# Layer 0 of a two-layer attention block: projection with two image buffers, V stored straight to its column strips

## The chip, the cores and the metric

The kernel runs on one core of a Trainium2 chip: TensorE (matmuls, clock 1.2 or 2.4 GHz as granted), VectorE, ScalarE, GpSimd, and SyncE (SP), which issues most DMAs. The metric is the time of one execution on the device in microseconds, the median of several. The profile shows one execution.

## What is computed

x is [4, 56, 56, 256]: four images of 3136 tokens with 256 channels. Layer 0 is a neighbourhood attention with 8 heads, queries and keys of rank 4, values of 32 channels per head and windows of 7 by 7; layer 1 is a full attention and a mixture of 8 experts.

```python
x = x + _L0_conv_ref(_gn(x), ...)        # group norm over 32 groups of 8 channels
...
q = (x @ Wq + bq).reshape(B, nh, H, W, lr) * scale
k = (x @ Wk + bk).reshape(B, nh, H, W, lr)
v = (x @ Wv + bv).reshape(B, nh, H, W, hd)
```

The reshape takes the 3136 x 32 numbers of an image as [8, 56, 56, 4] without moving them, so a head's grid is cut from 392 consecutive tokens: a token's channels are eight neighbouring columns (SUB = 8 times 4 for Q and K, 8 times 32 for V). Then softmax over the 49 neighbours with a relative bias, the mix with V, and a projection.

## The kernel before

Seven stages follow one another, each a block of its own, with a barrier between them. The change is in the first two.

`layer0_project` loops over four images with hardware loops (`Fori`). For each image SP loads x into one buffer `xs` (L170). TensorE turns it in 14 units of four transposes (L199), ScalarE copies each unit from PSUM into `xT` (L231), VectorE takes statistics of each (L247). Two tiny matmuls with the group matrix (L205) average over groups, VectorE and ScalarE make the inverse root (L62, L70, L64), and VectorE normalises `xT` in place in two instructions (L261). Then TensorE makes Q and K in 7 groups of 448 tokens (L211), which VectorE scales and splits into a high and a low part (L267, L270, L271; the high part is fp32r, and the later products use both), and V in 32 pieces of 98 tokens (L220), to which VectorE adds the bias (L275) into `vs`. SP stores Q/K as two arrays of 64 rows (L173, L174), V into `scratch_v` (L178), waits for all of it, and raises `image_done`, for which TensorE, ScalarE and VectorE wait at the end of the loop's body. Then it issues 14 copies inside HBM (L184) from `scratch_v` to `scratch_vw`: for each half of the heads and each of 7 overlapping strips of 14 columns, the strip's 56 rows of 7168 bytes. The load of the next image's x stands behind them in the same queue.

Beside this GpSimd writes the bias tables with DMAs of its own: fills of 9 MB with a huge number (L130), 24 small ones (L141), and 126 copies of window pieces (L153). Only attention reads these.

`layer0_attend` makes 8 iterations (two halves of the heads, four images) of 28 blocks. An iteration's Q and K are loaded by 32 DMAs (L350, L352) of 4 partitions x 8 pieces of 1568 bytes; GpSimd casts them into `qp` and `kp` (L414, L417). In the head of the stage GpSimd clears `qn` and `kn` (L420, L421), SP loads Q and K, the first biases (L364), the first values (L359) and then the identity `idn` (L402), for which TensorE waits before its first matmul (L440).

Of the kernel before, what the change touches and what calls it, by code (L numbers as in the profile page):

```python
# [6 lines left out]
F32 = mybir.dt.float32  # L7
# [3 lines left out]
ALU = mybir.AluOpType  # L11
# [5 lines left out]
N = H * W  # L17
# [55 lines left out]
def layer0_project(nc, A, S):  # L73
# [4 lines left out]

    with ExitStack() as ctx:
# [3 lines left out]
        def sem(name):  # L83
            return ctx.enter_context(nc.semaphore("p0_" + name))

        idn = sb("idn", [TT, TT])
        blk = sb("blk", [128, 128])
        wqk = sb("wqk", [128, CC, 64])
# [4 lines left out]
        xs = sb("xs", [TT, NT, C])  # L93
        xT = sb("xT", [128, CC, N])
# [6 lines left out]
        tmp = sb("tmp", [64, 2, GW])  # L101
# [9 lines left out]
        consts, loaded, turned, copied = sem("consts"), sem("loaded"), sem("turned"), sem("copied")  # L111
        stat, grouped, normed, chain = sem("stat"), sem("grouped"), sem("normed"), sem("chain")
        qk_made, qk_read, qk_split = sem("qk_made"), sem("qk_read"), sem("qk_split")
        v_made, v_read, stored, image_done = sem("v_made"), sem("v_read"), sem("stored"), sem("image_done")
        spread, rooted = sem("spread"), sem("rooted")
        rpb_loaded, filled = sem("rpb_loaded"), sem("tables_ready")
        tables_written, relaid, steps = sem("tables_written"), sem("relaid"), sem("steps")
        CHAIN = 5 + NG
        VT = 32
# [4 lines left out]
        def _(pool):  # L124
            pool.wait_ge(filled, 1)
# [7 lines left out]
            pool.wait_ge(filled, 2)  # L133
# [23 lines left out]
        @block.sync  # L157
        def _(sp):
            sp.dma_start(rp[:, :], A["rpb"].rearrange("h a b -> (h a) b")).then_inc(rpb_loaded, 16)
            for dst, src in ((idn[:, :], A["eye"][0:TT, 0:TT]), (blk[:, :], A["group_mean"]),  # L160
                             (wqk[:, :, 0:32], A["Wq0"].rearrange("(c p) n -> p c n", p=128)),
                             (wqk[:, :, 32:64], A["Wk0"].rearrange("(c p) n -> p c n", p=128)),
                             (wv[:, :, :], A["Wv0"].rearrange("(c p) n -> p c n", p=128)),
                             (bqk[0:32, :], A["bq0"].rearrange("(p a) -> p a", a=1)),
                             (bqk[32:64, :], A["bk0"].rearrange("(p a) -> p a", a=1)),
                             (sqk[:, :], A["qk_scale"]),
                             (bvb[:, :], A["bv0"].rearrange("(a n) -> a n", a=1).to_broadcast([TT, C]))):
                sp.dma_start(dst, src).then_inc(consts, 16)
            with sp.Fori(0, B) as b:
                sp.dma_start(xs[:, :, :], A["x"][b].rearrange("(j p) c -> p j c", p=TT)).then_inc(loaded, 16)  # L170

                sp.wait_ge(qk_split, (b + 1) * NG)
                sp.dma_start(S["qk0"][b, 0], qkh[:, :].bitcast(F32)).then_inc(stored, 16)  # L173
                sp.dma_start(S["qk0"][b, 1], qkl[:, :].bitcast(F32)).then_inc(stored, 16)  # L174
                for g in range(2):
                    sp.wait_ge(v_read, b * VT + 16 * (g + 1))
                    sp.sem_inc(steps, 1)
                    sp.dma_start(S["v0"][b, g].rearrange("(m t s) d -> t m (s d)", m=4, s=SUB), vs[:, 4 * g:4 * g + 4, :])\  # L178
                      .then_inc(stored, 16)
                sp.wait_ge(stored, (b + 1) * 64)  # L180
                sp.sem_inc(image_done, 1)
                for g in range(2):
# [4 lines left out]
            sp.wait_ge(relaid, B * 2 * COL_BLOCKS * 16)  # L187

        @block.tensor
        def _(pe):  # L190
            pe.wait_ge(consts, 144)
            with pe.Fori(0, B) as b:
                pe.wait_ge(loaded, (b + 1) * 16)
                for k in range(CC * NG):
                    g, c = divmod(k, CC)
                    if k >= 4:
                        pe.wait_ge(copied, b * (CC * NG) + k - 3)
                    for u in range(4):
                        last = pe.transpose(PS[:, k % 4, TT * u:TT * u + TT], xs[:, 4 * g + u, 128 * c:128 * c + 128],  # L199
                                            idn[:, :])  # L200
                    last.then_inc(turned, 1)

                for w, what in enumerate((mv[:, :, 0], vv[:, :])):
                    pe.wait_ge(stat, b * 2 + w + 1)
                    pe.matmul(PS[:, 4 + w, 0:CC], blk[:, :], what, start=True, stop=True).then_inc(grouped, 1)  # L205
                pe.wait_ge(normed, (b + 1) * CC)
                for g in range(NG):
                    if g >= 4:
                        pe.wait_ge(qk_read, b * NG + g - 3)
                    for c in range(CC):  # L210
                        last = pe.matmul(PS[0:64, g % 4, 0:GW], wqk[:, c, :], xT[:, c, GW * g:GW * g + GW],  # L211
                                         start=(c == 0), stop=(c == CC - 1))
                    last.then_inc(qk_made, 1)
                for j in range(VT):
                    if j >= 4:
                        pe.wait_ge(v_read, b * VT + j - 3)
                    g, m, hh = j // 16, j // 4 % 4, j % 4
                    tok = HT * (4 * g + hh) + 98 * m
                    for c in range(CC):
                        last = pe.matmul(PS[0:98, 4 + j % 4, 0:C], xT[:, c, tok:tok + 98], wv[:, c, :],  # L220
                                         start=(c == 0), stop=(c == CC - 1))
                    last.then_inc(v_made, 1)
                pe.wait_ge(image_done, b + 1)

        @block.scalar
        def _(act):
            with act.Fori(0, B) as b:
                for k in range(CC * NG):
                    g, c = divmod(k, CC)
                    act.wait_ge(turned, b * (CC * NG) + k + 1)  # L230
                    act.activation(xT[:, c, GW * g:GW * g + GW], PS[:, k % 4, 0:GW], ACT.Copy).then_inc(copied, 1)  # L231
                root(act, rstd[:, :], spread, rooted, b + 1)
                act.wait_ge(image_done, b + 1)

        @block.vector
        def _(dve):
            dve.memset(idle[:, :], 0.0)
# [3 lines left out]
            dve.wait_ge(consts, 144)  # L241
            with dve.Fori(0, B) as b:
                ch = Count(dve, chain, b * CHAIN)
                for k in range(CC * NG):
                    g, c = divmod(k, CC)
                    dve.wait_ge(copied, b * (CC * NG) + k + 1)
                    last = dve.bn_stats(stats[:, c, g, :], xT[:, c, GW * g:GW * g + GW])  # L247
                ch.after(last)
                dve.tensor_copy(idle[:, 1:2], idle[:, 0:1])
                for c in range(CC):  # L250
                    last = dve.bn_aggr(mv[:, c, :], stats[:, c, :, :].rearrange("p g s -> p (g s)"))
                last.then_inc(stat, 1)
                dve.wait_ge(grouped, b * 2 + 1)
                ch.after(dve.tensor_copy(gm[:, :], PS[:, 4, 0:CC]))
                ch.after(dve.tensor_tensor(dd[:, :], mv[:, :, 0], gm[:, :], ALU.subtract))
                ch.after(dve.tensor_tensor(dd[:, :], dd[:, :], dd[:, :], ALU.mult))
                dve.tensor_tensor(vv[:, :], dd[:, :], mv[:, :, 1], ALU.add).then_inc(stat, 1)
                dve.wait_ge(grouped, b * 2 + 2)
                inverse_root(dve, ch, rstd[:, :], PS[:, 5, 0:CC], 1e-5, spread, rooted, b + 1)
                for c in range(CC):  # L260
                    dve.tensor_scalar(xT[:, c, :], xT[:, c, :], gm[:, c:c + 1], rstd[:, c:c + 1],  # L261
                                      ALU.subtract, ALU.mult).then_inc(normed, 1)
                for g in range(NG):
                    dve.wait_ge(qk_made, b * NG + g + 1)
                    t = tmp[:, g % 2, :]

                    dve.tensor_scalar(t, PS[0:64, g % 4, 0:GW], bqk[:, 0:1], sqk[:, 0:1], ALU.add, ALU.mult)\  # L267
# [1889 lines left out]
```

## Time and profile before

| | us |
|---|---|
| median of 3 runs | 7947.33 (7942.66 to 7951.0) |
| profiled execution, its own time | 7931.02 |
| its span in the trace | 7929.2 |
| projection of layer 0 (0 to 443.9) | 443.9 |
| head of attention, to its first matmul (443.9 to 490.2) | 46.3 |
| rest of attention (490.2 to 1324.0) | 833.8 |

A stretch of the trace is read like this: busy time of each engine, the share of full speed at which TensorE's clock was granted, the mean busy share of the 16 DMA engines, and what they moved. An "x" after an instruction is a count; records of one run of instructions are merged in the timeline, so a duration there is that of the run.

### The profile page before, as it was taken

The numbers are of one execution on the slowest core, as the hardware profiler recorded it, in microseconds if no ns is written. First come the engines' busy times: TensorE is split into PE (matmuls) and PEld (weight loads), VectorE is DVE, ScalarE is ACT, GpSimd is POOL, SyncE is SP. The second block draws the span as 40 slices with busy tenths as digits, with TensorE's granted clock in tenths as the row PEclk, the third lists the DMA queues.
The fourth block names the chain that finished last, engine by engine and source line by source line (L and its number), as shares of the span: only waits on it lengthen the run. The fifth ranks groups of instructions, "written<-read, shape, count | busy, mean of one in ns | idle before, by whom it ended". The sixth has DMA issues, their size and how long they took to land. (4 is left out here: it accounts for less than half of the span.)

```text
span 7929.2 us, 152182 instructions
## 1 busy us (share of the span) xinstructions
PE 7120.8 (90%) x47408; PEld 4323.5 (55%) x47408; DVE 5376.1 (68%) x12877; ACT 4022.7 (51%) x9367; POOL 3714.0 (47%) x2395
## 2 busy tenths in 40 slices
PE   4459998989999999999999999999999888709999
PEld 2347776655455455455455455455455334608888
DVE  3359997659977677677677677677677102618888
ACT  0049997220055655565565555555565664104444
POOL 4011111110066666666666666666666665365554
PEclk8779999995599999999999999999999999859999
DMA  5442323871001201211211211211211102611221
GB/s 158 137 118 68 98 70 93 253 234 44 13 23 30 64 24 38 58 26 36 57 34 28 60 36 26 57 35 33 59 30 37 28 3 67 205 33 56 62 57 31
DMA packets 403136, 519.85 MB, mean 66 GB/s; under 512 B 64096, under 2 KB 355474, under 8 KB 399063
## 3 DMA queue, kind: packets, MB, share of 16 engines
q1 hardware_dynamic: 379687, 469.02, 21.9%
q0 software_dynamic: 22640, 40.75, 1.9%
q8 instruction: 421, 6.90, 0.4%
q14 instruction: 388, 3.18, 0.1%
HBM read 339.07 MB, written 200.10 MB: 68 GB/s over the span
## 5 line engine op out<-in xcount | busy, mean ns | idle before, releaser
L1248 DVE TENSOR_REDUCE a_tops<-a_ps 128x1 f32<-128x448 f32 (+1 forms) x5600 | 3071.8, 612 | 1092.9 <-PE a_ps L1150 1075.2
L1371 POOL TENSOR_TENSOR a_added<-a_P 128x896 f32<-128x896 f32 x1344 | 2799.3, 2102 | 2095.8 <-ACT a_P L1348 2095.8
L1348 ACT ACTIVATE a_P<-a_ps 128x448 f32<-128x448 f32 (+1 forms) x5600 | 2656.6, 547 | 2123.5 <-PE a_ps L1219 2081.9
L1219 PE MATMUL a_ps<-a_qp,a_kp 98*128 98x448 f32 (+1 forms) x5600 | 2154.1, 400 | 104.2 <-ACT a_P L1348 77.2
L1150 PE MATMUL a_ps<-a_hk,a_hq 96*128 96x448 f32 (+1 forms) x4900 | 1818.4, 381 | 2.0 <-DMA a_hq<-scratch_q 1.9
L1219 PEld LDWEIGHTS a_ps<-a_qp,a_kp 98*128 98x128 f32 (+1 forms) x5600 | 1028.9, 187 | 1296.0 <-ACT a_P L1348 741.0
L1170 PE MATMUL a_ps<-a_P,a_vt 128*32 128x448 f32 (+1 forms) x11200 | 1335.1, 549 | 0.0
L1150 PEld LDWEIGHTS a_ps<-a_hk,a_hq 96*128 96x128 f32 (+1 forms) x4900 | 916.4, 187 | 263.6 <-DVE a_tops L1248 170.3
L1186 PE MATMUL a_ps<-a_added,a_ones 128*32 128x448 f32 x5376 | 649.0, 555 | 0.0
L1170 PEld LDWEIGHTS a_ps<-a_P,a_vt 128*32 128x32 f32 (+1 forms) x11200 | 290.1, 109 | 513.9 <-issue 386.4
L550 ACT ACTIVATE n_P<-n_sm,n_mx 112x280 f32<-112x280 f32 x896 | 467.9, 522 | 108.4 <-DVE n_mx L498 108.3
L1271 DVE RECIPROCAL a_sums<-a_sums 128x112 f32<-128x112 f32 x224 | 185.0, 835 | 488.8 <-ACT a_sums L1323 488.8
L451 PE MATMUL n_ps<-n_idn,n_P 112*98 112x112 f32 x2688 | 421.2, 267 | 10.2 <-DVE n_P L508 10.2
L448 PE MATMUL n_ps<-n_idn 112*112 112x112 f32 x1792 | 373.1, 291 | 30.7 <-ACT n_PTs L557 29.8
L498 DVE CUSTOM_DVE_ANT_0 n_sm<-n_ps,n_bias 112x280 f32<-112x280 f32 x896 | 349.2, 445 | 72.3 <-PE n_ps L440 48.7
L557 ACT ACTIVATE n_PTs<-n_ps 98x336 f32<-98x336 f32 x896 | 391.1, 437 | 2.6 <-PE n_ps L451 2.0
L1138 PE MATMUL a_ps<-a_kp,a_qp 96*128 96x448 f32 (+1 forms) x700 | 370.2, 726 | 22.4 <-DMA a_kp<-scratch_k 22.4
L414 POOL CAST n_qp<-n_qn 128x784 fp32r<-128x784 f32 x32 | 52.5, 1639 | 673.7 <-DMA n_kn<-scratch_qk 338.2
L508 DVE TENSOR_SCALAR n_P<-n_P,n_rc 112x280 f32<-112x280 f32 x896 | 334.2, 415 | 16.0
L1951 ACT ACTIVATE e_h<-e_ps,e_b 128x512 f32<-128x512 f32 (+1 forms) x256 | 172.0, 672 | 336.2 <-PE e_ps L1911 311.8
L1924 PE MATMUL e_ps<-e_w2h,e_hTh 128*128 128x256 f32 (+1 forms) x1024 | 295.4, 289 | 37.0 <-DVE e_widest L2033 37.0
L448 PEld LDWEIGHTS n_ps<-n_idn 112*112 112x112 f32 x1792 | 255.4, 183 | 112.5 <-ACT n_PTs L557 98.9
(195 smaller groups left out, 7787.2 us busy)
## 6 DMA issues: line engine op xcount, KB each, us to landing
a_qp<-scratch_q SPq DMA_DIRECT2D x168, 224.0 KB, 3.9
a_kp<-scratch_k SPq DMA_DIRECT2D x96, 320.0 KB, 5.5
a_hk<-scratch_k SPq DMA_DIRECT2D x84, 336.0 KB, 5.0
scratch_t<-o_ts SPq DMA_DIRECT2D x56, 448.0 KB, 5.5
scratch_vw<-scratch_v SPq DMA_DIRECT2D x56, 392.0 KB
n_vt<-scratch_vw SPq DMA_DIRECT2D x64, 343.0 KB
a_hq<-scratch_q SPq DMA_DIRECT2D x84, 200.0 KB, 3.2
e_w<-in_w SPq DMA_DIRECT2D x16, 1024.0 KB, 7.1
```

The lines of the kernel that those rows point to most:

```text
L448: pe.matmul(PS[0:TT, turn_bank(m), 384:384 + TT], idn[:, :], idn[:, :], start=True, stop=True)
L451: last = pe.transpose(PS[0:CHUNK, turn_bank(m), TT * c:TT * c + TT], P[:, m % RP, k0:k0 + CHUNK], idn[:, :])
L550: act.activation(P[:, m % RP, :], sm[:, m % 4, :], ACT.Exp, bias=mx[:, m % 8:m % 8 + 1], scale=-1.0, accum_out=rs[:, m % 8:m % 8 + 1]).the ...
L557: act.activation(PTs[:, m % 8, :], PS[0:CHUNK, turn_bank(m), 0:3 * TT], ACT.Copy).then_inc(copied, 1)
L1138: pe.matmul(PS[0:rows_of(t), i % FIRST_BANKS, 0:GW], qp[0:96, hh, 128 * t:128 * t + rows_of(t)], kp[0:96, hh, GW * k:GW * k + GW], start=T ...
L1150: pe.matmul(PS[0:rows_of(t), MAX + i % MAXES, 0:GW], hq[:, 128 * t:128 * t + rows_of(t)], hk[:, GW * k:GW * k + GW], start=True, stop=True ...
L1170: last = pe.matmul(PS[HD * hh:HD * hh + HD, MIX, 0:GW], vt[0:rows, t, HD * hh:HD * hh + HD], P[0:rows, (2 * n + hh // 2) % (2 * RING), hh ...
L1186: last = pe.matmul(PS[HD * hh:HD * hh + HD, SUM, 0:GW], ones[:, :], added2[:, (2 * (PAIRS * j + u) + hh // 2) % 6, hh % 2, :], start=(u == ...
L1219: pe.matmul(PS[0:rows_of(t), i_s % 3, 0:GW], kp[0:98, hh, 128 * t:128 * t + rows_of(t)], qp[0:98, hh, GW * j:GW * j + GW], start=True, sto ...
L1248: dve.tensor_reduce(tops[0:rows_of(t), KT * hh + t, k:k + 1], PS[0:rows_of(t), bank, 0:GW], AX_X, ALU.max).then_inc(topped, 1)
L1348: act.activation(P[0:rows_of(t), (2 * n + pair) % (2 * RING), hh % 2, :], PS[0:rows_of(t), (4 * n + hh) % 3, 0:GW], ACT.Exp).then_inc(expe ...
L1371: pool.tensor_tensor(added2[:, a % 6, :, :], P[:, (2 * n + pair) % (2 * RING), :, :], P[:, (2 * n + 2 + pair) % (2 * RING), :, :], ALU.add ...
```

## The change

In `layer0_project` the loops over images are written out, and the images overlap. `xs` and `xT` have two buffers each. TensorE, ScalarE and VectorE go through 39 items per image (7 groups of Q/K, 32 pieces of V), and between an image's items stand the transposing units of the next (at odd items), its statistics (items 28 to 34) and its normalising (items 35 and 36). The transposes have two PSUM banks, Q/K two, V three. ScalarE makes the high part of Q/K (Identity with bias), VectorE the low part in one instruction. The scale goes into the weights once, and the weights' columns are put in another order, so that Q/K rows come out by rank component first. Q/K are stored by five DMAs of 32 rows (Q: high, low; K: high, low, high), V by 19 DMAs for each half of the heads, from `vs` straight into the strips; `scratch_v` is not used here any more. Each load of x is two DMAs. GpSimd begins its tables when image 0 is there. At the end the semaphores are cleared and a barrier is added. No engine waits for a whole image to be stored: ScalarE and VectorE wait for the stores of the buffer that they write next.

In `layer0_attend` Q and K come by 16 DMAs of 8 rows, the identity is loaded first, `qn` is cleared by VectorE while GpSimd clears `kn`, and the first loads of Q/K and biases don't wait for the clearing of `vt`.

```diff
@@ layer0_project
-        xs = sb("xs", [TT, NT, C])
-        xT = sb("xT", [128, CC, N])
+        xs = sb("xs", [TT, 2, NT, C])
+        xT = sb("xT", [128, 2, CC, N])
...
         def _(pool):
-            pool.wait_ge(filled, 1)
+            pool.wait_ge(filled, 2)
+            for h in range(2):
+                pool.wait_ge(loaded[0][h], 16)
...
+            def load(b):
+                if b >= 2:
+                    sp.wait_ge(turned, UNITS * (b - 1))
+                for h, (j0, j1) in enumerate(HALVES):
+                    sp.dma_start(xs[:, b % 2, j0:j1, :], A["x"][b, TT * j0:TT * j1, :].rearrange("(j p) c -> p j c", p=TT))\
+                      .then_inc(loaded[b % 2][h], 16)
+            def store_qk(b):
+                sp.wait_ge(qk_split, NG * (b + 1))
+                for qk in range(2):
+                    rows = slice(32 * qk, 32 * qk + 32)
+                    for term in range(2 + qk):
+                        src = (qkh, qkl)[term % 2]
+                        sp.dma_start(S["qk0"][b, qk, :, term].rearrange("h c s t -> (c s) h t"),
+                                     src[rows, :].rearrange("p (h t) -> p h t", h=NH).bitcast(F32)).then_inc(qk_stored, 16)
+            def store_values(b, g):
+                sp.wait_ge(v_read, b * VT + 16 * (g + 1))
+                for tc, xb, s0, s1, at in STRIP_PARTS:
+                    sp.dma_start(S["vw"][b, g, tc].rearrange("(m r c) d -> r m (c d)", m=4, c=14)
+                                 [:, :, 128 * at:128 * (at + s1 - s0)],
+                                 vs[xb:98:COL_BLOCKS, 4 * g:4 * g + 4, 128 * s0:128 * s1]).then_inc(v_stored[g], 16)
...
+            load(1)
+            for b in range(B):
+                if b + 2 < B:
+                    load(b + 2)
+                store_qk(b)
                 for g in range(2):
-                sp.wait_ge(stored, (b + 1) * 64)
-                sp.sem_inc(image_done, 1)
-                    for tc in range(COL_BLOCKS):
-                        sp.dma_start(S["vw"][b, g, tc].rearrange("(r c) d -> r c d", c=14),
-                                     S["v0"][b, g].rearrange("(r c) d -> r c d", c=W)[:, KEY_COL[tc]:KEY_COL[tc] + 14, :])\
-                          .then_inc(relaid, 16)
+                    store_values(b, g)
...
+            for b in range(B):
+                pe.wait_ge(normed, CC * (b + 1))
+                for n in range(ITEMS):
+                    if n < NG:
+                        queries_and_keys(b, n)
+                    else:
+                        value(b, n - NG)
+                    if b + 1 < B:
+                        if n % 2 == 1 and n < 2 * UNITS:
+                            turn(b + 1, n // 2)
+                        if n == 30:
+                            group(b + 1, 0)
+                        if n == 32:
+                            group(b + 1, 1)
...
+            def high_of(b, g):
+                n = NG * b + g
+                if g == 0 and b > 0:
+                    act.wait_ge(qk_stored, 16 * 5 * b)
...
+            def value(b, j):
+                n = VT * b + j
+                if j % 16 == 0 and b > 0:
+                    dve.wait_ge(v_stored[j // 16], V_STORES * b)
...
+    nc.clear_and_free_semaphores(sems)
+    nc.all_engine_barrier()
@@ layer0_attend
-                    for term in range(4):
-                        rows = slice(32 * hh + 4 * term, 32 * hh + 4 * term + 4)
-                        sp.dma_start(qn[rows, :, :], S["qk0"][b, term // 2, 0:32, tok:tok + HT]
-                                     .rearrange("(s c) t -> c s t", c=LR)).then_inc(loaded, 16)
...
+                    for half in range(2):
+                        rows = slice(32 * hh + 8 * half, 32 * hh + 8 * half + 8)
+                        sp.dma_start(qn[rows, :, :], S["qk0"][b, 0, 4 * g + hh, 0:2].rearrange("e c s t -> (e c) s t"))\
+                          .then_inc(loaded, 16)
...
-            sp.wait_ge(zeroed, 3)
+            sp.dma_start(idn[:, :], A["eye"][0:TT, 0:TT]).then_inc(consts, 16)
+            sp.wait_ge(zeroed, 2)
             load_qk(0, 0)
             load_bias(0, 0)
+            sp.wait_ge(padded, 1)
             load_values(0, 0, 0)
-            sp.dma_start(idn[:, :], A["eye"][0:TT, 0:TT]).then_inc(consts, 16)
```

## Rows read from the trace of the kernel before

**Rows 1.** Stretches: start:end, length, busy time, clock, DMA share, GB/s.
```profile
core 0: us, PE busy (x) PEld busy (x) DVE busy (x) ACT busy (x) POOL busy (x), PEclk, DMA share, GB/s
0.00:50.80 50.80, 0.00 (x0) 0.00 (x0) 2.25 (x3) 1.28 (x1) 9.54 (x16) 1.00 0.83 255
...
256.80:322.40 65.60, 49.46 (x216) 33.63 (x216) 38.25 (x78) 8.24 (x16) 0.00 (x0) 0.86 0.25 73
322.40:357.00 34.60, 0.04 (x1) 0.04 (x1) 0.00 (x0) 1.28 (x1) 0.00 (x0) 0.50 0.85 255
...
443.90:490.20 46.30, 0.02 (x4) 0.02 (x4) 1.55 (x1) 1.28 (x1) 14.39 (x9) 0.50 0.47 110
490.20:1324.00 833.80, 789.37 (x10644) 629.43 (x10645) 765.02 (x3352) 768.89 (x2678) 93.73 (x58) 0.96 0.29 76
```
**Rows 2.** Waits, 0 to 480 us: in total, times, longest.
```profile
PE p_ps L199 <- DMA p_xs<-in_x: 182.7, 4, 50.8
```
**Rows 3.** Groups of instructions by line and shape, 0 to 900 us.
```profile
L153 POOL DMA_DIRECT2D scratch_bias<-scratch_toeplitz x126 | 72.7, 586 | 10.8 <-issue 9.4 <-DMA scratch_toeplitz<-p_rn 1.4
L275 DVE TENSOR_TENSOR p_vs<-p_ps,p_bvb 98x256 f32<-98x256 f32 x128 | 53.1, 422 | 48.3 <-PE p_ps L220 48.3
...
L247 DVE BATCH_NORM_STATS2 p_stats<-p_xT 128x6 f32<-128x448 f32 x56 | 31.8, 617 | 186.5 <-ACT p_xT L231 184.2
...
L261 DVE TENSOR_SCALAR p_xT<-p_xT,p_gm,p_rstd 128x3136 f32<-128x3136 f32 x8 | 14.9, 1909 | 0.1
```
**Rows 4.** Timeline of the projection: start, duration, engine, line, count.
```profile
4.55 7.38 POOL L130 DMA_DIRECT2D scratch_bias<-p_far  x8
...
50.82 8.34 PE L199 MATMUL p_ps<-p_idn,p_xs 112*128 112x112 f32 x56 [50.82 <-DMA p_xs<-in_x]
...
68.09 13.45 PE L211 MATMUL p_ps<-p_xT,p_wqk 128*64 128x448 f32 x28 [4.46 <-DVE p_xT L261]
...
81.47 27.87 PE L220 MATMUL p_ps<-p_wv,p_xT 128*98 128x256 f32 x128
...
360.25 4.96 ACT L231 ACTIVATE p_xT<-p_ps 128x448 f32<-128x448 f32 x11 [0.20 <-PE p_ps L199]
...
373.89 12.45 PE L211 MATMUL p_ps<-p_xT,p_wqk 128*64 128x448 f32 x28 [4.46 <-DVE p_xT L261]
```
**Rows 5.** Short stretches: Q/K store, V store, x load, first Q/K load.
```profile
85.50:92.00 6.50, 6.50 (x32) 4.98 (x31) 3.29 (x8) 0.00 (x0) 0.68 (x2) 1.00 1.06 222
97.00:102.50 5.50, 5.50 (x28) 4.18 (x27) 2.58 (x7) 0.00 (x0) 5.50 (x11) 1.00 0.90 294
...
345.00:356.00 11.00, 0.00 (x0) 0.00 (x0) 0.00 (x0) 0.00 (x0) 0.00 (x0) 0.50 0.99 239
...
449.00:468.00 19.00, 0.00 (x0) 0.00 (x0) 0.00 (x0) 0.00 (x0) 0.35 (x1) 0.50 0.25 62
```
**Rows 6.** SP's issues by line: min/median/max of one in ns.
```profile
L178 SPq DMA_DIRECT2D scratch_v<-p_vs x8: 327/348/388, 96.2 to 414.9; - x8
...
L184 SPq DMA_DIRECT2D scratch_vw<-scratch_v x56: 798/802/982, 118.5 to 436.1; - x56
...
L350 SPq DMA_DIRECT2D n_qn<-scratch_qk x128: 249/404/1709, 449.4 to 1153.0; - x128
```
**Rows 7.** The next stage's high and low parts: min/median/max in ns.
```profile
L766 ACT ACTIVATE o_high<-o_ps,o_bqk x112: 633/633/636, 1370.7 to 1763.1; 128x448 fp32r<-128x448 f32 x112
L823 DVE SCALAR_TENSOR_TENSOR o_low<-o_ps,o_bqk,o_high x112: 670/682/685, 1371.4 to 1763.8; 128x448 fp32r<-128x448 f32 x112
```
**Rows 8.** Timeline of attention's head.
```profile
444.00 2.71 POOL L420 MEMSET n_qn<- 128x3136 f32 x1 [298.01 <-POOLq L79]
...
449.38 0.28 SPq L350 DMA_DIRECT2D n_qn<-scratch_qk  x1
...
481.17 1.57 POOL L414 CAST n_qp<-n_qn 128x784 fp32r<-128x784 f32 x1 [31.81 <-DMA n_kn<-scratch_qk]
...
483.35 1.83 SPq L402 DMA_DIRECT2D n_idn<-in_eye  x1
...
490.18 0.58 PE L440 MATMUL n_ps<-n_kp,n_qp 16*112 16x280 f32 x4 [76.03 <-DMA n_idn<-in_eye]
```

More of the change, by code:

```diff
@@ L73, in layer0_project @@
 def layer0_project(nc, A, S):
+    sems = []
     with ExitStack() as ctx:
@@ L83, in sem @@
         def sem(name):
-            return ctx.enter_context(nc.semaphore("p0_" + name))
+            sems.append(nc.alloc_semaphore("p0_" + name))
+            return sems[-1]
+        UNITS = CC * NG
+        VT = 32
+        ITEMS = NG + VT
+        TURN, MEAN, QK, VAL = 0, 2, 3, 5
         idn = sb("idn", [TT, TT])
         blk = sb("blk", [128, 128])
+        raw = sb("raw", [128, CC, 64])
         wqk = sb("wqk", [128, CC, 64])
@@ L189, in _ @@
+            for g in range(2):
+                sp.wait_ge(v_stored[g], V_STORES * B)
+            sp.wait_ge(qk_stored, 16 * (B * 5))
         @block.tensor
         def _(pe):
[L191 to L223, printed above, removed]
@@ new lines, in turn @@
+            def turn(b, k):
+                g, c = divmod(k, CC)
+                if k == 0:
+                    pe.wait_ge(loaded[b % 2][0], 16 * (b // 2 + 1))
+                if k == CC * 4:
+                    pe.wait_ge(loaded[b % 2][1], 16 * (b // 2 + 1))
+                if b * UNITS + k >= 2:
+                    pe.wait_ge(copied, b * UNITS + k - 1)
+                for u in range(4):
+                    last = pe.transpose(PS[:, TURN + k % 2, TT * u:TT * u + TT], xs[:, b % 2, 4 * g + u, 128 * c:128 * c + 128],
+                                        idn[:, :])
+                last.then_inc(turned, 1)
@@ new lines, in group, with queries_and_keys @@
+            def group(b, w):
+                pe.wait_ge(stat, b * 2 + w + 1)
+                pe.matmul(PS[:, MEAN, CC * w:CC * w + CC], blk[:, :], (mv[:, :, 0], vv[:, :])[w], start=True, stop=True)\
+                    .then_inc(grouped, 1)
+            def queries_and_keys(b, g):
+                n = NG * b + g
+                if n >= 2:
+                    pe.wait_ge(qk_split, n - 1)
+                for c in range(CC):
+                    last = pe.matmul(PS[0:64, QK + n % 2, 0:GW], wqk[:, c, :], xT[:, b % 2, c, GW * g:GW * g + GW],
+                                     start=(c == 0), stop=(c == CC - 1))
+                last.then_inc(qk_made, 1)
@@ new lines, in value @@
+            def value(b, j):
+                n = VT * b + j
+                if n >= 3:
+                    pe.wait_ge(v_read, n - 2)
+                g, m, hh = j // 16, j // 4 % 4, j % 4
+                tok = HT * (4 * g + hh) + 98 * m
+                for c in range(CC):
+                    last = pe.matmul(PS[0:98, VAL + n % 3, 0:C], xT[:, b % 2, c, tok:tok + 98], wv[:, c, :],
+                                     start=(c == 0), stop=(c == CC - 1))
+                last.then_inc(v_made, 1)
@@ new lines, in _ @@
+            pe.wait_ge(consts, CONSTS)
+            for k in range(UNITS):
+                turn(0, k)
+            group(0, 0)
+            group(0, 1)
+            pe.wait_ge(prepared, PREPARED)
+            for b in range(B):
[12 more added lines that the diff above has]
+                            group(b + 1, 1)
@@ L225, in _, with take_turned @@
         @block.scalar
         def _(act):
[L227 to L233, printed above, removed]
+            def take_turned(b, k):
+                g, c = divmod(k, CC)
+                act.wait_ge(turned, b * UNITS + k + 1)
+                act.activation(xT[:, b % 2, c, GW * g:GW * g + GW], PS[:, TURN + k % 2, 0:GW], ACT.Copy).then_inc(copied, 1)
@@ L235, in _, with collect @@
+            for b in range(B):
+                for n in range(ITEMS):
+                    if n < NG:
+                        high_of(b, n)
+                    if b + 1 < B:
+                        if n % 2 == 1 and n < 2 * UNITS:
+                            take_turned(b + 1, n // 2)
+                        if n == 33:
+                            root(act, rstd[:, :], spread, rooted, b + 2)
         @block.vector
         def _(dve):
+            ch = Count(dve, chain, 0)
+            def collect(b, k):
+                g, c = divmod(k, CC)
+                dve.wait_ge(copied, b * UNITS + k + 1)
+                last = dve.bn_stats(stats[:, c, g, :], xT[:, b % 2, c, GW * g:GW * g + GW])
+                if k == UNITS - 1:
+                    ch.after(last)
@@ new lines, in means, with spreads @@
+            def means(b):
+                dve.tensor_copy(idle[:, 1:2], idle[:, 0:1])
+                for c in range(CC):
+                    last = dve.bn_aggr(mv[:, c, :], stats[:, c, :, :].rearrange("p g s -> p (g s)"))
+                last.then_inc(stat, 1)
+            def spreads(b):
+                dve.wait_ge(grouped, b * 2 + 1)
+                ch.after(dve.tensor_copy(gm[:, :], PS[:, MEAN, 0:CC]))
+                ch.after(dve.tensor_tensor(dd[:, :], mv[:, :, 0], gm[:, :], ALU.subtract))
+                ch.after(dve.tensor_tensor(dd[:, :], dd[:, :], dd[:, :], ALU.mult))
+                dve.tensor_tensor(vv[:, :], dd[:, :], mv[:, :, 1], ALU.add).then_inc(stat, 1)
@@ new lines, in variances, with invert, normalise @@
+            def variances(b):
+                dve.wait_ge(grouped, b * 2 + 2)
+                dve.tensor_scalar(rstd[:, :], PS[:, MEAN, CC:2 * CC], 1e-5, None, ALU.add).then_inc(spread, 1)
+            def invert(b):
+                dve.wait_ge(rooted, b + 1)
+                ch.after(dve.reciprocal(rstd[:, :], rstd[:, :]))
+            def normalise(b, c):
+                dve.tensor_scalar(xT[:, b % 2, c, :], xT[:, b % 2, c, :], gm[:, c:c + 1], rstd[:, c:c + 1],
+                                  ALU.subtract, ALU.mult).then_inc(normed, 1)
@@ new lines, in _ @@
+            dve.tensor_tensor(bqk[:, :], bqk[:, :], sqk[:, :], ALU.mult).then_inc(prepared, 1)
+            dve.wait_ge(prepared, PREPARED)
+            invert(0)
+            for c in range(CC):
+                normalise(0, c)
+            for b in range(B):
+                for n in range(ITEMS):
+                    if n < NG:
+                        low_of(b, n)
+                    else:
+                        value(b, n - NG)
+                    if b + 1 < B:
+                        if n % 2 == 1 and n < 2 * UNITS:
+                            collect(b + 1, n // 2)
+                        if n == 28:
+                            means(b + 1)
+                        if n == 30:
+                            spreads(b + 1)
+                        if n == 32:
+                            variances(b + 1)
+                        if n == 34:
+                            invert(b + 1)
+                        if n in (35, 36):
+                            normalise(b + 1, n - 35)
```

140 lines of the change are left out of this document (68 added, 72 removed).

## Prediction

> **What bounds the kernel now.** I read the stretches of the span first [rows 1]. The change touches the first 490 us only: projection from 0 to 443.9, and the head of attention, until TensorE's first matmul at 490.2. The rest of attention (833.8 us, TensorE busy 789, ScalarE 769, VectorE 765) and all after it keep their code. The projection alternates: a stretch with no DMA to speak of (256.8 to 322.4, 65.6 us, DMA share 0.25) and one in which every engine stands still and only DMAs run (322.4 to 357.0, 34.6 us, 0.04 us of matmuls, DMA share 0.85). Nothing overlaps, because `image_done` holds TensorE, ScalarE and VectorE until V is stored, and the next image is loaded behind the 14 copies of V into strips. The waits say the same: TensorE waited 182.7 us for `p_xs` over four images [rows 2], and 76.0 us before the first matmul of attention [rows 8]. So the stage is bound by a chain of latencies, and what decides is which engine or queue is the longest when an image's work overlaps the next one's.
>
> **The time before the first projection.** Before, the 8 fills of the bias tables (9.0 MB) go out at 4.55 us, x (3.2 MB) behind them, and TensorE starts at 50.8 [rows 1, 4]. Now GpSimd waits for image 0. 3.21 MB of x at the 239 GB/s that a load alone got [rows 5] are 13.4 us; from an issue at 1.7, with 2 us of latency, 17 us; the constants are queued behind it (0.5 MB, 2 us): TensorE starts at 19 (17 to 23). From there to the first Q/K matmul it was 68.09 - 50.82 = 17.3 us [rows 4]. Two PSUM banks for the transposes instead of four let TensorE run only one unit ahead of ScalarE's copy, and scaling the weights adds five tiny instructions: I add 1.5 us (0.5 to 3). First Q/K matmul at 37.8.
>
> **One image in the steady state, engine by engine.** TensorE: 28 Q/K records; at the full clock one takes its place every 0.373 us (image 3 did 28 in 12.45 us with a part at the low clock; image 0 13.45) [rows 4], so 10.4 us. V: 128 records in 27.87 us, 0.218 apart [rows 4]. The 14 transposing units: 11 copies of them ran in 4.96 us once the clock was up, 0.45 each [rows 4], so 6.3. Statistics matmuls 0.9. 28 changes between the kinds of work, at 0.05 us as an estimate, 1.4 (0 to 3). VectorE: 14 x 0.617 statistics, 2 x 1.909 normalising, 7 x 0.68 for the low parts (the nearest row is the same operation in the next stage), 32 x 0.422 V, 2 us of small ones: 32.7 us [rows 3, 7]. Three of its instructions a Q/K group become one, and ScalarE takes the high part at 0.63 [rows 7]. ScalarE: 14 x 0.45 + 7 x 0.63 = 10.7 us and two table loads. So TensorE is the longest, with one stall that I can place: the two normalising instructions of the next image stand at items 35 and 36 of VectorE's order. From TensorE's end of item 35, VectorE needs 0.2 + 2 x (0.42 + 1.91) = 4.9 us before `normed` is full; TensorE has three more values of 0.87 us, so it stands for 2.3 us. Sum: 10.4 + 27.9 + 6.3 + 0.9 + 1.4 + 2.3 = 49.2 us. In the Q/K phase two banks return in 0.63 + 0.68 + some 0.4 of semaphores = 1.7 us, within the 1.9 us of a matmul group and a transposing unit; no stall.
>
> **Is the queue longer?** An image is x 3.21 MB at 239 GB/s = 13.4 us; Q and K, now five stores of 0.40 MB, 2.0 MB at the 222 GB/s that the 64-row stores got = 9.0; V written straight, 7 strips x 56 rows x 7168 bytes x 2 = 5.62 MB, at the 294 GB/s of the V store [rows 5] 19.1 us. Together 41.5 us, against 49.2 of TensorE: hidden, with 8 us to spare. The rows know no store that reads only 14 partitions. From below it is the 294; from above the pace of the slowest load here: the first Q/K load of attention, 1.6 MB over a quarter of the DMA engines (share 0.25), took 449.4 to 481.2 [rows 5, 8], 12.6 GB/s per engine; at that, 14 engines give 177 GB/s, 31.8 us, and the queue comes to 54.2. I take 294, since the V store is nearest (SBUF to HBM, rows of 4 KB against now 1.5 to 4 KB). Issuing: 38 strip stores an image; the V store took 0.35 us to issue, a strip copy 0.80 [rows 6]. At 0.5 this is 19 us of SP, at 0.8 it is 30: below 49 either way.
> A rule speaks against the narrow stores. The Trainium skill, "SBUF — State Buffer", section on Door 1, says that a DMA's rate goes by how many of 16 ports its partitions reach, and that rows 0 to 63 reach no more than 0 to 31. The trace agrees with the half rate for 64 rows (222 GB/s at full DMA share), and by the rule 32 rows cost no more: the 9.0 us stand.
>
> **Order of waits.** SP now queues per image: load(b+2), five Q/K stores, 19 strip stores, 19 more. load(b+2) waits for the transposes of image b, done before image b's items begin, so nothing is held up behind it. ScalarE's `high_of(b+1, 0)` waits for Q/K stores issued some 36 us earlier; VectorE's value(b+1, 0) for strips issued some 27 us earlier that need 10. Image 1 is the tight one: x(1) shares the DMA with the 9 MB of fills. In that company 3.2 MB of x were there only at 50.8 before, some 44 us for them [rows 1, 4]; now x(1) runs from about 17, so its first half is there at some 40, when the first transposing unit wants it (37.8 + 3), and the second at 61, when unit 8 does. GpSimd's 126 small copies (72.7 us of its time before, [rows 3]) follow the fills and 24 smaller ones and end near 155, hidden by the stage. No stall taken; 0 to 8 us as bounds.
>
> **The stage.** 37.8; image 0 49.2 + 3.0 for the low clock of its first matmuls [rows 4] = 90.0; two more 49.2 = 188.4; the last has no next image, 10.4 + 27.9 + 0.5 = 38.8: 227.2. Then 19 strip stores (2.8 MB, 9.6 us of data, 9.5 of issue) and landing, 14 us together (9 to 20, at 0.35 to 0.8 a store, plus what queues before them): 241.2. Clearing semaphores and one more barrier: 1.5 (0 to 3): 242.7. Before 443.9: a gain of 201.2.
>
> **Head of attention.** Before, 46.3 us: two memsets of GpSimd (5.4), 32 loads, casts from 481.2, and only then the identity, issued at 483.4 behind biases and values, which TensorE waited for [rows 8]. After: one memset per engine (2.7 plus 0.3), 16 loads of 8 rows. 4-row loads kept a quarter of the DMA engines busy; 8-row loads should use half, so 1.6 MB take between 9.5 (21 GB/s per engine, as in the V store) and 31.8 us (no gain); I take 13, as rows of 12.5 KB replace pieces of 1568 bytes. Four casts of at most 1.57 are 5.8 us. TensorE is ready at 3.2 + 13 + 5.8 = 22; the biases, whose four loads are next in the queue, at about 23. Gain 23.3 (5 to 28).
> The Trainium skill, "DMA: Bandwidth & Descriptors", section on why a DMA increments its semaphore by 16, says that the engine count divides the slowest dimension, 4 then and 8 now; the share of 0.25 agrees. The rule on ports, taken by itself, would give 8 rows two ports of 27 GB/s, 30 us, and with it the second rival's time; 4 rows would then have had one, and 62 GB/s was measured [rows 5].
>
> **Sum.** 201.2 + 23.3 = 224.5 us. The profiled execution took 7931.0 (7929.2 in the span) and would take 7706.5; the timed runs had a median of 7947.3, 16 above, so 7723.
>
> **Rivals.** (1) The strip stores run slower than the V store, the queue becomes the bound: 54.2 instead of 49.2 for three images, in the tail 6 us more, and bubbles between waits and issue, 5 us an image: 15 + 6 + 15 = 36 more, 7759. For it: source rows on only 14 partitions. Against: 14 DMA engines already carried the V store. (2) The head's load is no faster: 18 us more, 7742. For it: it was slower in the head than its engines' share explains. (3) Slower than before: an overlapped stage waits for its strips at every image. The whole gain of 224 us over four images is 56 each, so an image must take 105 us, and a strip store (105 - 13.4 - 9.0)/38 = 2.2 us instead of 0.5; it decides from there. Only the worst issue of a 49 KB load comes near, 1.71 us, and its median is 0.40 [rows 6]. At 2.5 us each: 38 x 0.3 x 4 = 46 more than before, 7993. (4) The overlap doesn't come about, TensorE waiting each image for VectorE's normalising and the transposes: 65 us an image, 3 x 16 = 48 more, 7771; nothing in the order asks for it.
>
> **Chances.** Forecast 0.57, (1) 0.20, (2) 0.14, (4) 0.06, (3) 0.03. A change within 0.2% (16 us), about what this kernel's timing can't tell from none, has no case of its own: 0.01. Faster 0.96, slower 0.03. Range: down to 7697 (head 5, tail 5, changes of work and start 8, runs 8); up to 7780, which takes in (1) with (2) in part, and (4). The forecast's own: 7700 to 7745.
>
> **What would show it.** First transposes at 19 us; images 49 us apart at the Q/K matmuls; TensorE's only regular wait 2.3 us on VectorE's normalising; DMA share near 0.85; attention's first matmul 22 to 24 us after its memset; attention from there still 834 us. Wrong would be: TensorE, ScalarE or VectorE waiting for `qk_stored` or `v_stored`, transposes waiting for x, or a longer attention body.

## The result

The changed kernel took 7744.6 us in the median (7731.4 to 7755.7, four runs) beside 7945.0 before: a ratio of 0.9746 (95% interval 0.9729 to 0.9764), 200 us less. In a second comparison it took 7729.2 (five runs) beside 7935.1: 0.9739 (0.9726 to 0.9753), 206 us less. The forecast of 7723, 224 less, had the direction and lies 22 us under the first median and 6 under the second; both medians lie inside the stated range. The profiled execution took 7755.7 us, span 7753.8, the longest of its four.

The stretches of the changed kernel's profile show where the time came from (columns as in [rows 1]): two images, the last image, the wait for its stores, and the head of attention.

```profile
87.70:134.90 47.20, 45.22 (x216) 30.08 (x216) 30.13 (x65) 11.94 (x22) 43.73 (x74) 1.00 0.87 237
134.90:182.10 47.20, 45.22 (x216) 30.07 (x216) 30.13 (x65) 11.93 (x22) 22.88 (x42) 1.00 0.72 205
182.10:221.90 39.80, 39.03 (x156) 24.45 (x156) 18.88 (x41) 4.40 (x7) 0.00 (x0) 1.00 0.62 182
221.90:247.90 26.00, 0.00 (x0) 0.00 (x0) 0.00 (x0) 0.00 (x0) 0.00 (x0) 0.58 0.47 167
...
247.90:287.50 39.60, 0.00 (x0) 0.02 (x1) 4.22 (x2) 1.28 (x1) 8.68 (x6) 0.50 0.76 100
```

Where a compute stretch of 65.6 us alternated with a DMA stretch of 34.6 [rows 1], an image now takes 47.2 us, TensorE works in 45.2 of them, its clock stays at full speed, and the DMAs run beside it. In the timeline the same kernel's steps show at their edges:

```profile
20.67 4.71 PE L236 MATMUL p_ps<-p_idn,p_xs 112*128 112x112 f32 x24 [20.67 <-DMA p_bqk<-in_bk]
...
39.22 4.55 PE L250 MATMUL p_ps<-p_xT,p_wqk 128*64 128x448 f32 x8 [4.76 <-DVE p_xT L348]
...
87.74 3.22 PE L250 MATMUL p_ps<-p_xT,p_wqk 128*64 128x448 f32 x8 [1.97 <-DVE p_xT L348]
...
182.12 8.14 PE L250 MATMUL p_ps<-p_xT,p_wqk 128*64 128x448 f32 x20 [1.97 <-DVE p_xT L348]
```

The Q/K matmuls of an image begin 48.5, 47.2 and 47.2 us apart. In front of the first image's TensorE waits 4.76 us for VectorE's normalising, in front of each of the other three 1.97 us, and after the first image the projection has no longer wait of TensorE. Then the head of attention, which answers to [rows 8]:

```profile
247.93 2.71 POOL L552 MEMSET n_kn<- 128x3136 f32 x1 [90.15 <-POOLq L410]
...
251.35 0.27 SPq L481 DMA_DIRECT2D n_qn<-scratch_qk  x1
...
281.54 1.57 POOL L546 CAST n_qp<-n_qn 128x784 fp32r<-128x784 f32 x1 [30.89 <-DMA n_kn<-scratch_qk]
...
287.51 0.58 PE L571 MATMUL n_ps<-n_kp,n_qp 16*112 16x280 f32 x4 [66.30 <-POOL n_kp L549]
```

TensorE now waits for the casts (66.3 us, with the tail of the projection in it), not for the identity. But the load still takes 251.4 to 281.5, 30.2 us, where the old one took 31.8. And the strip stores show in SP's issues (min/median/max of one in ns) with a median of 782 ns:

```profile
L195 SPq DMA_DIRECT2D scratch_vw<-p_vs x152: 781/782/2967, 71.1 to 243.9; - x152
```

In time order, SP's issues from image 1's strip stores on look like this:

```profile
121.04 39.56 SPq L195 DMA_DIRECT2D scratch_vw<-p_vs  x38
160.64 0.53 SPq L189 DMA_DIRECT2D scratch_qk<-p_qkh  x1
...
167.86 34.74 SPq L195 DMA_DIRECT2D scratch_vw<-p_vs  x38
...
209.84 34.84 SPq L195 DMA_DIRECT2D scratch_vw<-p_vs  x38
```

SP issues without a gap from 71.1 to 244.7 us. The x load (image 1 only), the five Q/K stores and the 38 strip stores take it 55.7 us for image 1 and 42.0 each for images 2 and 3, against TensorE's 47.2. So SP is behind when an image's values end: image 1's last strip store is issued 26 us after TensorE has gone on to image 2's Q/K, and VectorE's first write into the second half of `vs` (165.7) comes only 5 us after the last store of the old contents was issued (160.6). No engine waits for the stores, but with little to spare.

So two questions stand: why the head kept 16.6 us of what was forecast to go, and why the tail took 26 us instead of 15.5.

### The profile page after: what moved, and what is told of

The parts are those of the page before. It is cut to its first block and busy times, and to the rows that moved or that the text cites. A ratio compares the mean times of both kernels' runs of the same rounds, so it can differ in the third digit from the quotient of the medians.

```text
span 7753.8 us, 151401 instructions
## 1 busy us (share of the span) xinstructions
PE 7122.0 (92%) x47408; PEld 4321.3 (56%) x47408; DVE 5352.3 (69%) x12827; ACT 4036.6 (52%) x9389; POOL 3715.9 (48%) x2394
## 3 DMA queue, kind: packets, MB, share of 16 engines
q1 hardware_dynamic: 380887, 457.79, 22.7%
```

## The experiments

All variants start from the changed kernel. Stage times are of one profile each.

**Q/K rows four partitions apart.**

```diff
-                        rows = slice(32 * hh + 8 * half, 32 * hh + 8 * half + 8)
+                        rows = slice(32 * hh + half, 32 * hh + 32, 4)
...
-                    rows = slice(32 * hh, 32 * hh + 16)
+                    rows = slice(32 * hh, 32 * hh + 32)
```

> The changed kernel, but the 8 rows of a Q/K load of attention go to partitions four apart (32 hh + half + 4 j) instead of 8 neighbours, and the score matmuls contract over 32 rows, of which the other 16 are zero. Same bytes, same 8 rows and 16 DMAs. Theory A (the load is held by how few SBUF ports its neighbouring rows reach): the head load, 30.2 us in the changed kernel (251.4 to 281.5), takes 9 to 14 us, and the time from attention's memset to its first matmul falls from 39.6 to 20 to 25 us. Theory B (8 of 16 DMA engines, or the read from HBM, hold it): it stays within 3 us of 30 and the head at 37 to 41. Attention's body must keep its pace in both.

Measured: 7696.4 us in one run (before, beside it: 7930.2). The timeline of this variant:

```profile
253.89 0.69 SPq L481 DMA_DIRECT2D n_qn<-scratch_qk  x1
...
268.20 1.57 POOL L546 CAST n_qp<-n_qn 128x784 fp32r<-128x784 f32 x1 [15.03 <-DMA n_kn<-scratch_qk]
...
274.18 0.58 PE L571 MATMUL n_ps<-n_kp,n_qp 32*112 32x280 f32 x4 [50.95 <-POOL n_kp L549]
```

The load takes 253.9 to 268.2, 14.3 us, and from the memset at 250.5 to the first matmul 23.7. Bytes, number of DMAs and source are those of the changed kernel; for the load only where the rows lie in SBUF differs. (That the matmuls contract over 32 rows doesn't shorten the head: a run below has that edit alone, with a head of 40.2.) The biases and values are queued behind the Q/K loads, in the changed kernel from 256.8 on, so its 30.2 us are in part spent in their company. These stretches lie before that company, from 2 us after the first issue: neighbouring rows, then rows four apart.

```profile
253.40:256.70 3.30, 0.00 (x0) 0.00 (x0) 0.00 (x0) 0.00 (x0) 0.00 (x0) 0.50 0.49 61
```

```profile
255.90:264.30 8.40, 0.00 (x0) 0.00 (x0) 0.00 (x0) 0.00 (x0) 0.00 (x0) 0.50 0.43 143
```

At nearly the same share of busy DMA engines, about 8 of 16, twice as much moves. Theory A stands as far as it says that the place of the rows decides. The Trainium skill, "SBUF — State Buffer", section on Door 1, has four neighbouring partitions share one port of 27 GB/s; by it 8 neighbours reach two, 1.6 MB in 30 us as an estimate, and rows four apart reach eight. The trace agrees with the direction. That the first comes out at 30.2 us is in part luck: of the changed kernel's load, 251.4 to 256.7 moved 76 GB/s with nothing beside it, more than two ports of 27, and the rest ran beside biases and values. Of the 14.3 us, 10.4 are SP's issues, so this run doesn't show what eight ports would give. The issue itself, 0.30 us for neighbouring rows, costs 0.60 with a step:

```profile
L481 SPq DMA_DIRECT2D n_qn<-scratch_qk x64: 602/603/1532, 253.9 to 919.1; - x64
```

**32 loads of 4 neighbouring rows.** The inner loop runs over four terms again, with rows of 12.5 KB.

```diff
-                    for half in range(2):
-                        rows = slice(32 * hh + 8 * half, 32 * hh + 8 * half + 8)
+                    for term in range(4):
+                        rows = slice(32 * hh + 4 * term, 32 * hh + 4 * term + 4)
```

> The changed kernel, but Q and K of attention come by 32 DMAs of 4 neighbouring rows (12.5 KB each) instead of 16 of 8. Theory A (ports): 4 neighbours reach half of what 8 reach, so the head load takes 55 to 62 us and the head some 65 to 70. Theory B (DMA engines, 4 instead of 8): also about twice, 55 to 60. Theory C (the pieces of 1568 bytes were as fast as rows of 12.5 KB, and the old load's 31.8 us are what any such load takes here): 30 to 34 us. With the first kernel this separates rows in memory from rows in SBUF.

Measured: 7728.1 us in one run. The load took 253.9 to 282.4, 28.5 us, the head 37.9. A stretch with Q/K loads alone, then a line of this kernel's timeline:

```profile
255.90:264.60 8.70, 0.00 (x0) 0.00 (x0) 0.00 (x0) 0.00 (x0) 0.00 (x0) 0.50 0.23 53
```

```profile
282.37 1.57 POOL L544 CAST n_qp<-n_qn 128x784 fp32r<-128x784 f32 x1 [29.20 <-DMA n_kn<-scratch_qk]
```

The DMA share is 0.23, half of the 0.49 with 8 rows, and the rate 53 GB/s against 61. Neither A nor B: half the DMA engines and half the neighbours are nearly as fast as twice of each. C's time is nearest. So the forecast's reading of the share 0.25 (twice the DMA engines, and so well under half the time) is wrong in this place: the load was not bound by them. This run answers another rival of the run above too: its 32 issues also take 10.7 us and put the biases off by as much as the stepped issues do, and the load stays at 28.5 us, so the later biases are not what halved it. That ports are what binds is argued, not shown: why 4 rows, which by the same rule have one port, do as well as 8 stays open. A possible reason is that loads of different groups of four are under way at once; no run parts that.

**The last strips from two queues.** First ScalarE issued 28 of the last image's 38 strip stores and SP 10:

```diff
+            for g in range(2):
+                act.wait_ge(v_read, (B - 1) * VT + 16 * (g + 1))
+                for tc, xb, s0, s1, at in (STRIP_PARTS, STRIP_PARTS[1::2])[g]:
+                    act.dma_start(S["vw"][B - 1, g, tc]...
```

> The changed kernel, but of the last image's 38 strip stores ScalarE's queue issues the 19 of the first half and 9 of the second, SP the other 10. Theory A (the tail, 26.0 us from the last value to attention's memset, is bound by SP's issues at 0.82 us each, 29 of them still to go): it falls to 11 to 14 us, the stage ends near 235. Theory B (bound by the data or by DMA engines): it stays within 3 us of 26.

Measured: 7723.5 us in one run; the last value at 220.3 and attention at 239.0, a tail of 18.7 us instead of 26.0. It fell by less than A had it (11 to 14), but well out of B's 3 us. ScalarE's 28 took 29.2 us, 1.04 each, so ScalarE's queue now set the end, with SP done at 231:

```profile
206.54 29.16 ACTq L319 DMA_DIRECT2D scratch_vw<-p_vs  x28
```

Then both queues took every other strip store, in both halves (`STRIP_PARTS[0::2]` and `[1::2]`):

> The changed kernel with the last image's strip stores taken in turns by SP and ScalarE in both halves, and nothing else. The same edit in the kernel with spread rows had its attention memset at 236.7 us, 15.0 after the last value. Expected here 235 to 238, head 38 to 41, and 10 to 12 us less than the changed kernel's 7729.2: 7717 to 7720. If the body's length hangs on when the last strips land, it shows here as well (body under 832).

Measured: 7716.2 us (7703.7 to 7733.4, four runs), ratio 0.9721 (0.9703 to 0.9740) to the kernel before, which took 7937.1. Attention begins at 236.0, a tail of 13.4 after the last value, at 222.6, and the head takes 39.9. The tail was bound by issues. Beside each other the two queues took 22.7 us for 38 stores, 0.60 a store, where SP alone took 34.8. The body of attention (first to last matmul) took 847.0 us, so earlier strips don't shorten it.

**Images in turn.** The transposes, statistics and normalising of an image stand after the previous one's items on every engine, here on TensorE:

```diff
-                    if b + 1 < B:
-                        if n % 2 == 1 and n < 2 * UNITS:
-                            turn(b + 1, n // 2)
...
+            for b in range(B):
+                for k in range(UNITS):
+                    turn(b, k)
```

> The changed kernel with its two buffers, narrow stores and strips, but an image's transposes, statistics and normalising come after the previous image's items, in turn, not between them. It tells what the interleaving is worth beside no longer waiting for stores and loads. Theory A (most of the gain is the DMA waits that went, 35 us an image): an image takes 38.8 + 17 to 18.5 = 56 to 58 us instead of 47.2, the stage ends 27 to 33 us later, near 277. Theory B (the queue would show as soon as the engines have gaps, or the low clock after the gaps costs more): 62 us an image or more, the stage ends after 295.

Measured: 7749.0 us in one run. Attention begins at 276.4. A stretch of 57 us is about an image (columns as in [rows 1]); TensorE works 48.3 of it at a clock of 0.91, in the two stretches behind it as well, and the Q/K matmuls begin 58 us apart (97.3, 155.2, 213.1).

```profile
58.00:115.00 57.00, 48.29 (x213) 30.78 (x213) 31.18 (x63) 11.47 (x22) 42.94 (x74) 0.91 0.84 223
```

Theory A stands. Of the projection's 196 us (443.9 to 247.9), 167 come without any interleaving: 30 of them from the start, where the first transpose comes at 20.6 instead of 50.8, and some 137 mainly from images that no longer wait for stores and loads (TensorE's waits for x after the first were 182.7 - 50.8 = 131.9 us [rows 2]). The interleaving adds 28.5.

**V through HBM, but overlapped.** Two stores and 14 copies inside HBM instead of 38 strip stores:

```diff
-                for tc, xb, s0, s1, at in STRIP_PARTS:
-                    sp.dma_start(S["vw"][b, g, tc]...
+                sp.dma_start(S["v0"][b, g].rearrange("(m t s) d -> t m (s d)", m=4, s=SUB), vs[:, 4 * g:4 * g + 4, :])
...
+            def relay(b, g):
+                sp.wait_ge(v_stored[g], 16 * (b + 1))
+                for tc in range(COL_BLOCKS): ...
```

> The changed kernel with its overlap, but V goes as before: two stores of an image's V to HBM, and 14 copies inside HBM from there into the strips, which SP issues once the store has landed. Theory A (strips straight from SBUF matter little while TensorE sets the pace): images stay 47 to 49 us apart and only the tail changes. Theory B (the extra 3.2 MB and the copies make the queue the bound: x 13.4, Q/K 9.0, V store 11, copies 21.5, together 55 us): images 55 us apart, ScalarE or VectorE waiting for stores or transposes for x, the stage 15 to 25 us longer than the changed kernel's 247.9. The fewer issues (14 at 0.8 and 2 at 0.35 instead of 38 at 0.8) speak for A, the bytes for B.

Measured: 7737.2 us in one run. Q/K matmuls begin at 38.0, 87.5, 134.7 and 183.6: 49.5, 47.2 and 48.9 us apart, and attention at 249.5. The stretches show the price that does not reach the time, a DMA share of 1.00 and 0.87 in images that have 0.87 and 0.72 with strips:

```profile
90.00:137.00 47.00, 45.03 (x214) 29.87 (x213) 30.11 (x64) 11.31 (x21) 36.58 (x62) 0.98 1.00 284
137.00:185.00 48.00, 46.03 (x218) 30.26 (x217) 30.11 (x64) 11.94 (x22) 24.41 (x44) 0.99 0.87 293
```

Theory A: the stage ends 1.6 us later, inside the scatter of profiles of the same projection code (246.6 to 250.5), so the direct strip stores as such are worth nothing that this run shows. They unload the DMA engines; they don't carry the gain. B's 55 us an image didn't come: its terms had rates of 239 to 294 GB/s [rows 5], and these stretches move 284 to 293.

**Tables first.**

```diff
-            for h in range(2):
-                pool.wait_ge(loaded[0][h], 16)
```

> The changed kernel, but GpSimd starts its table fills at once, not when image 0 is there. Theory A (x shares the DMA engines with 9 MB of fills as in the kernel before): the first transpose starts at 38 to 47 us instead of 20.7, and the stage ends by nearly as much later, 265 to 274. Theory B (x is now issued before the fills and keeps ahead of them): 22 to 28 us, and the stage ends within 6 us of 248.

Measured: 7748.7 us in one run. The first transpose starts at 44.0 instead of 20.7, and attention at 270.1 instead of 247.9: 22.2 us for two lines.

```profile
43.97 9.94 PE L234 MATMUL p_ps<-p_idn,p_xs 112*128 112x112 f32 x56 [43.97 <-DMA p_bqk<-in_bk]
```

What TensorE waited for last is the constants, as in the changed kernel, not x. x is issued at 1.6 us and the fills from 4.6 on; the constants are issued behind x until 37.6, where the changed kernel had issued them by 15.8. Theory A's time came, but how much of it is x and how much the constants this run doesn't part.

**Both remedies together, and the changed kernel again.**

> The changed kernel with the Q/K rows of attention four partitions apart and the last image's strip stores taken in turns by SP and ScalarE, in both halves. From the single runs: head 39.6 to 23.7 us, tail 26.0 to 18.5 with an uneven split (ScalarE 28, SP 10); an even split ends both queues at about 231 and the stage at 234 to 236. Sum 28 to 31 us less than the changed kernel's median 7744.6: 7712 to 7718. If the data and not the issues bound the tail by now (share of the DMA engines 0.8 in it), the stage ends at 238 to 240 and the time is 7720.

Measured: 7683.0 us (7680.6 to 7695.1, five runs), ratio 0.9683 (0.9670 to 0.9696) to the kernel before; beside it on the same chip the changed kernel took 7729.2. That is 46 us less, and 62 less than the 7744.6 from which 28 to 31 were expected.

> The changed kernel again, beside the one above on the same chip. Every theory: median within 10 us of 7744.6, stage end 246 to 250, head 38 to 41 us. The length of attention's body (840.7 in the kernel before, 851.4 in the changed one, 828.9 to 839.1 in four variants that leave it alone or nearly) falls between 828 and 852 if that difference is scatter from run to run, and near 851 if it belongs to the change.

Its stage: attention at 246.6, first matmul at 286.4. With both remedies:

```profile
236.71 0.35 SPq L535 DMA_DIRECT2D n_idn<-in_eye  x1
...
260.10 0.58 PE L577 MATMUL n_ps<-n_kp,n_qp 32*112 32x280 f32 x4 [39.02 <-POOL n_kp L555]
```

From 286.4 to 260.1 are 26 us, a little less than expected. In the body of attention, 828.2 us against 842.4, are 14 more. Of the two profiled executions one is 34 us shorter than the other, so the medians' 46 are not accounted for in full. To part the two edits of the spread rows, the 32-row matmuls were run with the neighbouring loads:

> The changed kernel, Q/K loads of attention to neighbouring rows as it has them, but the score matmuls contract over 32 rows, of which 16 are zero. It parts the two edits of the spread kernel, whose attention body took 828.9 and 828.2 us in two profiles, where eight profiles with neighbouring rows gave 832.3 to 851.4. Theory A (the slow Q/K load of the next iteration sits before the values in the queue and makes TensorE late and its clock fall): body 832 to 851, head 38 to 41. Theory B (32 live rows a matmul keep the clock up, or change the pace): body 826 to 831. Time by A within 10 us of 7729, by B some 12 less.

Measured: 7721.9 us (7717.1 to 7736.9, four runs), ratio 0.9732 (0.9716 to 0.9749); body 838.0, head 40.2. So the rows of the matmul don't bring the short body. In the nine profiles with neighbouring rows in the new layout the body took 832.3 to 851.4, in the two with spread rows 828.9 and 828.2. The timed runs speak for the faster load as well: the kernel with both remedies and the one with the even tail alone differ only by the two edits of the spread rows, and their medians by 33 us (7683.0 and 7716.2, no run of one within the range of the other), of which the head explains 16.5. TensorE's waits in the body of the changed kernel's second profile, then of the kernel with both remedies (in total, times, longest):

```profile
PE n_ps L594 <- issue: 3.9, 1, 3.9
PE n_ps L579 <- issue: 2.1, 1, 2.1
```

```profile
PE n_ps L585 <- ACT n_PTs L695: 31.7, 31, 2.1
```

The first has gaps in which TensorE waited for nothing that the profile shows; the second has none. Eight of the nine profiles with neighbouring rows have two or three such gaps, which begin 12 to 30 us after an iteration's Q/K load began to be issued (in this one loads at 404.2 and 718.3, gaps at 421.0 and 735.9). The granted clock over the body is 0.95 in the two longest (851.4 and 847.0) and 0.97 in the two with spread rows. But the slow load alone doesn't make the gaps: the run with 4 rows, whose load takes 28.5 us, has none, a clock of 0.97 and a body of 832.3, and the kernel before had none and a body of 840.7. What makes them stays open.

## Why the prediction was right, and where its terms were off

- *The start of the first image.* 19 forecast, 20.7 measured; Q/K at 37.8 forecast, 39.2 measured. Right, and that the tables wait for image 0 is worth 22 us.
- *An image.* 49.2 forecast, 47.2 measured; the stall 2.3 forecast, 1.97 measured. The working by engines was right. No row stood behind the 1.4 us for 28 changes between kinds of work, and they cost nothing that I can see. The first image took 48.5 instead of 52.2: its low clock cost little, as it ended during the first Q/K groups. The last value came at 221.9, where the sum had 227.2.
- *The queue is hidden.* Right in the outcome: DMA share 0.87 and 0.72, and no engine waits for `qk_stored` or `v_stored`. Rival (1) didn't come. But the 8 us to spare were worked out from bytes. In issues it counted the strip stores alone, 19 to 30 us an image; with the Q/K stores and x SP needed 42.0 to 55.7. The Q/K stores, which were to be issued some 36 us ahead of ScalarE's next write, were issued 16 ahead (167.9 and 183.9), and the stores of the old contents of `vs` 5 ahead of VectorE's.
- *The tail.* The first of two failed terms: 14 and 1.5 us forecast, 26.0 measured, 10.5 too little. The step was "19 strip stores (2.8 MB, 9.6 us of data, 9.5 of issue)": with 0.5 us a store and nothing queued before them, SP would be done with the first half when the last value came. In its place the trace shows SP with 28 of 38 stores to go. They took 23.0 us, 0.82 each, about the upper bound of 0.80 that the prediction had. That price alone would leave some 21 of them: the values of the first half were ready at 207.9 us, but SP still issued image 3's Q/K stores until 209.8 (five in 7.2 us, which the sum had at nothing), and its first ten strip stores then took 11.8 us. From the last issue to attention's memset are 3.2 us, landing, clearing and barriers together; no run parts the 1.5 us forecast for the last two. The even split over two queues gave 12.6 us of the tail back.
- *The head.* The second failed term: 23.3 forecast, 6.7 gained (46.3 to 39.6), 16.6 too little. The failed step is "8-row loads should use half, so 1.6 MB take between 9.5 ... and 31.8 us (no gain); I take 13". It read the share of busy DMA engines as the limit. The engines did double (share 0.25 before, 0.49 to 0.53 now) and the time hardly moved. What decides is where the rows lie in SBUF: 30.2 us for neighbours, 14.3 four apart. Rival (2) came true. The two-port time of 30 us, which the prediction weighed against one measured rate and set aside, was the nearer one, in part by luck, as the rates above show. The identity, first in the queue, and the parallel memsets gave the 6.7 us.
- *The sum.* 242.7 + 23.0 = 265.7 to attention's first matmul forecast, 287.5 and 286.4 measured. That is 21.8 too late in the first: 27.1 from tail and head, less 5.3 from the images, whose error had the other sign. Measured to the first matmul the gain is 202.7 and 203.8 us, which is nearly all of the 200 and 206. What is left is within the scatter of the stages that didn't change: the body of attention 851.4 and 842.4 in two profiles of the same program. (The body goes to TensorE's last matmul, 840.7 us before the change; the 833.8 that the prediction carries over stops at 1324.0, some 7 us before it.) That the second median comes within 6 us of 7723 is luck: the forecast started from 7947.3, and the kernel before took 7935.1 beside it.

## What to carry to other kernels

Where every engine stands still at the end of each iteration for a store, take the wait for "everything stored" away first: here that gave most of 167 us, the earlier start 30 of them, and the fine interleaving 28. A DMA to a few neighbouring partitions can be slow, and twice as many busy DMA engines didn't help it here; putting the same rows four partitions apart halved it, at the cost of a dearer issue. Add up the issues of every DMA in a queue, at the price of the nearest row of the same shape, and compare the sum with the time of an image: a queue that is as long as the engines' work stands behind them at the end of the stage, where nothing covers it.

## What the runs showed that was not expected

- The same load to 8 rows costs SP 0.30 us to issue with neighbouring rows and 0.60 with rows four apart. A strip store of 14 rows seven apart, of another shape and direction, costs 0.78.
- Loads of 4 and of 8 neighbouring rows take nearly the same time (28.5 and 30.2 us for 1.6 MB), on half as many busy DMA engines.
- The body of attention took 832 to 851 us with neighbouring rows and 828 and 829 with spread ones, more than its own first load explains. Why isn't shown.
